# Third attention of a graph network: edge logits from a node table by one-hot products, value rows gathered over three stages

## What is computed

```python
h = (x @ W).reshape(N, HEADS, HEAD_DIM)
a_src = jnp.einsum('nhd,hd->nh', h, att_src)
a_dst = jnp.einsum('nhd,hd->nh', h, att_dst)
e = a_src[src] + a_dst[dst]
e = jax.nn.leaky_relu(e, NEG_SLOPE)
m = jax.ops.segment_max(e, dst, num_segments=N)
e = jnp.exp(e - m[dst])
denom = jax.ops.segment_sum(e, dst, num_segments=N)
alpha = e / denom[dst]
msg = alpha[:, :, None] * h[src]
out = jax.ops.segment_sum(msg, dst, num_segments=N)
return out.reshape(N, HEADS * HEAD_DIM) + bias
```

## Time and profile before

| what | us |
|---|---|
| median of 3 runs | 6803.33 (6801.85 to 6805.95) |
| the profiled execution | 6809.68 |
| its span in the trace | 6807.9 |
| logits of the third attention (`edge_logits`) | 4129 to 4657 |
| its `segment_max` and `bulk` | 4657 to 4712 |
| its `edge_sum` | 4712 to 4962 |

### The profile page before, as it was taken

The page is one execution under the profiler, slowest core; times in us unless marked ns, Lnnn a source line. Parts: engine busy times, 40 slices in busy tenths (PEclk is TensorE's granted clock), DMA queues, the critical chain, the costliest instruction groups (busy, mean ns, idle before and its releaser), DMA issues. The chain is left out here.

```text
span 6807.9 us, 82209 instructions
## 1 busy us (share of the span) xinstructions
PE 4906.5 (72%) x21980; PEld 3937.2 (58%) x21981; DVE 2933.0 (43%) x7123; ACT 1436.9 (21%) x3790; POOL 3441.3 (51%) x3131
## 2 busy tenths in 40 slices
PE   3877486998656486999996754333926588688858
PEld 2777365776444264888886654333626466566645
DVE  5655674323444474101102022114752477567754
ACT  1000482332000192000000221002913122122221
POOL 1777685777577481000000235774833377667710
PEclk8555697999877698999997875556958799789978
DMA  3999461001699673444453546884716388678810
GB/s 116 355 345 323 134 222 46 1 1 18 231 336 339 205 244 100 125 126 125 128 147 102 185 144 193 236 236 152 241 64 201 106 267 260 197 229 261 265 48 24
DMA packets 802690, 1204.72 MB, mean 177 GB/s; under 512 B 102860, under 2 KB 589677, under 8 KB 802313
## 3 DMA queue, kind: packets, MB, share of 16 engines
q1 hardware_dynamic: 365913, 512.77, 25.5%
q0 software_dynamic: 141376, 372.59, 18.8%
q10 hardware_dynamic: 295152, 316.45, 13.2%
HBM read 832.49 MB, written 368.52 MB: 176 GB/s over the span
## 5 line engine op out<-in xcount | busy, mean ns | idle before, releaser
L630 POOL DMA_INDIRECT logit_rows<-tab,src_a x832 | 825.9, 993 | 308.9 <-issue 230.5
L1900 POOL DMA_INDIRECT max_rows<-tab,src_r x784 | 741.1, 945 | 366.6 <-issue 220.3
L749 PE MATMUL ps_a<-msg,sel 128*128 128x264 f32 (+2 forms) x2496 | 621.9, 400 | 132.3 <-DVEq L681 72.2
L1571 POOL DMA_INDIRECT moe_x<-xn,slot x100 | 97.2, 972 | 1219.2 <-POOLq L96 1189.3
L379 POOL DMA_INDIRECT counts<-put_n,put_at x400 | 560.8, 1402 | 215.7 <-issue 135.0
L749 PEld LDWEIGHTS ps_a<-msg,sel 128*128 128x128 f32 x2496 | 454.2, 192 | 299.7 <-DVE acc L695 85.6
L1121 PE MATMUL ps_a<-hl,blocks 128*128 128x256 f32 x2600 | 578.1, 380 | 0.5 <-PE ps_a L1121 0.3
L1121 PEld LDWEIGHTS ps_a<-hl,blocks 128*128 128x128 f32 x2600 | 493.1, 190 | 76.9 <-issue 13.6
L660 POOL TENSOR_TENSOR msg<-edge_rows,extra 128x1024 f32<-128x1024 f32 x208 | 394.0, 1904 | 198.5 <-DMA edge_rows<-slot_rows 124.0
L630 POOL DMA_INDIRECT logit_rows<-tab_kv,src_a x416 | 395.8, 952 | 177.5 <-issue 117.0
L2006 DVE TENSOR_TENSOR_SCAN run<-same,run,ps_t 128x512 f32<-128x512 bf16 x392 | 479.1, 1265 | 0.8 <-PE ps_t L1941 0.8
(11 more groups left out here) (434 smaller groups left out, 9115.0 us busy)
## 6 DMA issues: line engine op xcount, KB each, us to landing
slot_rows<-logit_rows ACTq DMA_DIRECT2D x312, 512.0 KB
edge_rows<-slot_rows SPq DMA_DIRECT2D x312, 512.0 KB
blocks<-counts SPq DMA_DIRECT2D x390, 320.0 KB
seg_rows<-back ACTq DMA_DIRECT2D x196, 512.0 KB
counts<-zeros ACTq DMA_DIRECT2D x130, 320.0 KB
locs<-loc_slots SPq DMA_DIRECT2D x312, 128.0 KB
wf<-in_L_ffn_W SPq DMA_DIRECT2D x57, 512.0 KB
att<-in_attr_t SPq DMA_DIRECT2D x196, 128.0 KB
```

The costliest lines, as they stand in the source:

```text
L630: self.nc.gpsimd.indirect_dma_start(out=self.rows[:, (n % Q) * Q + j, :], out_offset=None, in_=table, in_offset=bass.IndirectOffsetOnAxis( ...
L749: nc.tensor.matmul(ps_a[:, n % 8, 0:C], sel[:, b % 2, j, :], rhs, start=True, stop=True).then_inc(summed, 1)
L1900: nc.gpsimd.indirect_dma_start(out=rows[:, b * Q + j, :], out_offset=None, in_=table, in_offset=bass.IndirectOffsetOnAxis(ap=g.src_r[:, n ...
```

## The change

`edge_logits` is no longer used by `gnn2`. In its place `table_logits` gets a_src of an edge without gathering a row. For a step it makes a one-hot `from_t` of the source's low 7 bits (from a new slot table `slo_slots`), and PE multiplies it with the whole node table `a_s`, 25 tiles by 4 heads: 100 columns. DVE then picks the tile that the source's high bits name (`choose`, against `lane`) and sums over the tiles (`gather_up`). ACT makes `from_t` in two instructions (|s - p|, then ReLU(1 - that)), DVE makes `sel_t` as before.

The rows h are still gathered, by the same 416 indirect DMAs, now of 256 numbers from `tab`, with SP storing each group to `slot_rows`. They are spread over three stages by `LATE = (66, 75)`: groups 0 to 65 in the logits stage, 66 to 74 in `segment_max`, 75 to 103 in the new `late_sum`, which takes the place of `edge_sum`. There POOL gathers 12 groups while DVE does all products of the first 24 groups; from group 24 on POOL does the product of each third group, and gathers one group ahead of it while any is left.

```diff
+LATE = (66, 75)
...
+                o.then(v.tensor_scalar(slo_i[:], ids_i[:, :, 0, :], P - 1, None, ALU.bitwise_and))
                 o.link(v.tensor_copy(ids_f[:], ids_i[:]))
+                o.link(v.tensor_copy(slo_h[:], slo_i[:]))
...
+class Late:
+    def gather(self, pool, n):
+        b = n % Q
+        if n >= Q:
+            pool.wait_ge(self.kept[b], 16 * (n // Q))
+        for j in range(Q):
+            self.nc.gpsimd.indirect_dma_start(
...
+            ).then_inc(self.got[b], 16)
+    def store(self, sp, n):
+        b = n % Q
+        sp.wait_ge(self.got[b], 64 * (n // Q) + 64)
+        sp.dma_start(self.g.slot_rows[n], self.rows[:, b * Q:(b + 1) * Q, :].rearrange("p j d -> p (j d)")).then_inc(self.kept[b], 16)
...
+def table_logits(nc, g, late, gathers, a_s, node_cols, logits, second):
...
+                for n in range(gathers):
+                    late.gather(pool, n)
...
+                for n in range(SG):
+                    b = n % Q
+                    if n >= Q:
+                        sp.wait_ge(sel_set, n - Q + 1)
+                    sp.dma_start(locs[:, b, :], ...
+                    if n >= Q:
+                        sp.wait_ge(far_set, n - Q + 1)
+                    sp.dma_start(slos[:, b, :], ...
+                    while kept < min(gathers - 1, (n - 6) * gathers // SG):
+                        late.store(sp, kept)
+                        kept += 1
...
+                    pe.wait_ge(sel_set, n + 1)
+                    pe.wait_ge(from_set, n + 1)
+                    if n >= 2:
+                        pe.wait_ge(chosen, n - 1)
+                        pe.wait_ge(summed, n - 1)
+                    for j in range(Q):
+                        nc.tensor.matmul(ps_a[:, n % 2, j * NT * H:(j + 1) * NT * H], from_t[:, n % 2, j, :], table, start=True, stop=True)
+                        ins = nc.tensor.matmul(ps_b[:, n % 2, j * P:j * P + 2 * H], sel_t[:, n % 2, j, :],
...
+                select(0)
+                for n in range(SG):
+                    if n + 1 < SG:
+                        select(n + 1)
+                    choose(n)
+                    if n:
+                        leak(n - 1)
+                    gather_up(n)
+                    add(n)
+                leak(SG - 1)
...
+def late_sum(nc, g, late, have, acc, extra, heads):
+    FIRST, AHEAD = 24, 12
+    by_pool = [n >= FIRST and n % 3 == 2 for n in range(SG)]
...
+                for n in range(SG):
+                    if n == FIRST - 1:
+                        for done in range(have, min(have + AHEAD, SG)):
+                            late.gather(pool, done)
+                        done = min(have + AHEAD, SG)
+                    if by_pool[n]:
+                        if done < SG:
+                            late.gather(pool, done)
+                            done += 1
+                        pool.wait_ge(rows_in[n % Q], 16 * (n // Q) + 16)
+                        if n >= 2:
+                            pool.wait_ge(summed, 4 * (n - 2) + 4)
+                        product(nc.gpsimd, n).then_inc(msg_p, 1)
...
+                multiply(0)
+                v.memset(acc[:, :, 0:C], 0.0).then_inc(zeroed, 1)
+                v.memset(odd[:], 0.0).then_inc(zeroed, 1)
+                dve.wait_ge(zeroed, 2)
+                for n in range(SG):
+                    if n + 1 < SG:
+                        multiply(n + 1)
+                    add(n)
...
-def segment_max(nc, g, logits, maxima, H, puts=(0, 0)):
+def segment_max(nc, g, logits, maxima, H, puts=(0, 0), late=None, gathers=(0, 0)):
...
+                    for n in range(*gathers):
+                        late.gather(pool, n)
...
-        node_rows(nc, g, [g.x], [(g.ins["L2_gnn_W"], 0, 0)], D + 8, None, [(0, D + 4, hw, g.tab4), (D + 4, D + 8, adst, None)], ln=True,
+        node_rows(nc, g, [g.x], [(g.ins["L2_gnn_W"], 0, 0)], D + 8, None,
+                  [(0, D, hw, g.tab), (D, D + 4, a_s, None), (D + 4, D + 8, adst, None)], ln=True,
...
-            edge_logits(nc, g, g.tab4, D + 4, cols, logits, 0, D, second=loop_e)
-            segment_max(nc, g, logits, shift, 4)
+            table_logits(nc, g, late, LATE[0], a_s[:], cols, logits, loop_e)
+            segment_max(nc, g, logits, shift, 4, late=late, gathers=LATE)
...
-        edge_sum(nc, g, None, acc, extra, heads=4)
+        late_sum(nc, g, late, LATE[1], acc, extra, heads=4)
```

More of the change, by code:

```diff
@@ L225, in slot_tables @@
         row_i = sb("row_i", [P, STEPS], I32)
+        slo_i, slo_h = sb("slo_i", [SPG, GROUPS, P], I32), sb("slo_h", [SPG, GROUPS, P], BF16)
         turned = ps("turned", [P, 2, 512])
@@ L243, in _ @@
                 sp.dma_start(g.loc_slots.rearrange("(g p l) -> p g l", g=GROUPS, l=P), loc_h[:]).then_inc(loc_out, 16)
+                sp.dma_start(g.slo_slots.rearrange("(g p l) -> p g l", g=GROUPS, l=P), slo_h[:]).then_inc(loc_out, 16)
                 sp.dma_start(g.dst_slots[1:SLOTS + 1].rearrange("(g p l) -> p g l", g=GROUPS, l=P),
@@ L255, in _ @@
                 sp.wait_ge(sent, 96)
-                sp.wait_ge(loc_out, 16)
+                sp.wait_ge(loc_out, 32)
             @block.vector
@@ L916, in _, with __init__ @@
                         ins.then_inc(made, 1)
-def segment_max(nc, g, logits, maxima, H, puts=(0, 0)):
+class Late:
+    def __init__(self, nc, ph, g):
+        self.nc, self.g = nc, g
+        self.rows = ph.sb("late_rows", [P, W, D], F32)
+        self.got = [ph.sem(f"late_got{b}") for b in range(Q)]
+        self.kept = [ph.sem(f"late_kept{b}") for b in range(Q)]
+    def gather(self, pool, n):
[4 more added lines that the diff above has]
+            self.nc.gpsimd.indirect_dma_start(
+                out=self.rows[:, b * Q + j, :], out_offset=None, in_=self.g.tab,
+                in_offset=bass.IndirectOffsetOnAxis(ap=self.g.src_a[:, n * Q + j:n * Q + j + 1], axis=0)
+            ).then_inc(self.got[b], 16)
[3 more added lines that the diff above has]
+        sp.dma_start(self.g.slot_rows[n], self.rows[:, b * Q:(b + 1) * Q, :].rearrange("p j d -> p (j d)")).then_inc(self.kept[b], 16)
@@ L947, in _ @@
                     put_counts(nc, g, pool, *puts)
+            if late is not None:
+                @block.gpsimd
+                def _(pool):
+                    for n in range(*gathers):
+                        late.gather(pool, n)
             @block.sync
@@ L953, in _ @@
                     sp.dma_start(cut[c * H:(c + 1) * H, :], at.partition_broadcast(H)).then_inc(cut_in, 16)
+                if late is not None:
+                    for n in range(gathers[0] - 1, gathers[1] - 1):
+                        late.store(sp, n)
                 sp.wait_ge(cut_in, 16 * C)
@@ L1808, in gnn2 @@
         sb = ph.sb
-        hw = sb("hw", [P, NT, D + 4], F32)
+        hw = sb("hw", [P, NT, D], F32)
         cols = sb("cols", [P, NT, 8], F32)
+        a_s = sb("a_s", [P, NT, 4], F32)
         extra = sb("extra", [P, STEPS, 9], F32)
-        adst, loop, a_s, rows = cols[:, :, 0:4], cols[:, :, 4:8], hw[:, :, D:D + 4], hw[:, :, 0:D]
-        node_rows(nc, g, [g.x], [(g.ins["L2_gnn_W"], 0, 0)], D + 8, None, [(0, D + 4, hw, g.tab4), (D + 4, D + 8, adst, None)], ln=True,
+        late = Late(nc, ph, g)
+        adst, loop, rows = cols[:, :, 0:4], cols[:, :, 4:8], hw[:]
+        node_rows(nc, g, [g.x], [(g.ins["L2_gnn_W"], 0, 0)], D + 8, None,
+                  [(0, D, hw, g.tab), (D, D + 4, a_s, None), (D + 4, D + 8, adst, None)], ln=True,
                   heads=(4, [g.ins["L2_gnn_att_src"], g.ins["L2_gnn_att_dst"]]))
-        bulk(nc, [("v", lambda v: v.tensor_add(loop, a_s, adst)),
+        bulk(nc, [("v", lambda v: v.tensor_add(loop, a_s[:], adst)),
                   ("v", lambda v: v.scalar_tensor_tensor(loop, loop, 0.2, loop, ALU.mult, ALU.max))])
@@ L1840, in gnn2 @@
                   ("v", lambda v: v.tensor_copy(g.seg_end[:], end[:].rearrange("p t a -> p (t a)"))),
-                  ("v", lambda v: v.tensor_tensor(a_s, loop, none[:].broadcast_to([P, NT, 4]), ALU.mult)),
-                  ("v", lambda v: v.tensor_add(shf, shf, a_s)),
+                  ("v", lambda v: v.tensor_tensor(a_s[:], loop, none[:].broadcast_to([P, NT, 4]), ALU.mult)),
+                  ("v", lambda v: v.tensor_add(shf, shf, a_s[:])),
                   ("v", lambda v: v.tensor_sub(loop, loop, shf)),
@@ L2437, in build @@
         g.loc_slots = dram("loc_slots", [SLOTS], BF16)
+        g.slo_slots = dram("slo_slots", [SLOTS], BF16)
         g.same_slots = dram("same_slots", [SLOTS], BF16)
@@ L2444, in build @@
         g.tab8 = dram("tab8", [NP_, D + 8])
-        g.tab4 = dram("tab4", [NP_, D + 4])
         g.slot_rows = dram("slot_rows", [STEPS // Q, P, Q * D])
```

188 lines of the change are left out of this document (added).

## The result

| | us |
|---|---|
| before, median of 4 runs | 6804.64 (6801.85 to 6808.52) |
| after, median of 4 runs | 6700.47 (6693.92 to 6706.78) |
| after / before | 0.9842, 95% interval 0.983 to 0.9854 |
| the profiled execution of after, and its span | 6706.78, 6705.0 |

A forecast was written before the change was run, and what follows sets the result against it. POOL's 416 gathers were taken to limit the logits stage, 520 of 528 us. Terms -162 + 20 + 43 + 3 = -96 took the profiled 6809.7 to 6714, or 6708 since that execution lay 6.35 above the median; range 6660 to 6778.

The forecast's parts named there:

- Step of PE, 3.45 us a group: Logits stage: weight loads set PE's step, 16 records at 0.215 us, so PE sets the pace at 3.45 us a group.
- Rival 3: Logits stage: PE steps as in the first attention's alternating 128- and 64-row weights, 4.19 us a group; total 6785; 8%.
- Rival 4: Logits stage: each wide record adds its stream to its weight load, 4.96 us a group; total 6864, slower; 3%.
- Clock 0.50: Logits stage: PE, though busy all the time, stays at clock 0.50, the 1.2 GHz level.
- rival 1: Logits stage: PE's clock goes up, POOL's 330 us become the bound, stage 338 us, total 6680; 25%.
- DVE beside PE, 2.4 to 2.9 us: Logits stage: DVE's one-hot, choosing, sum and hand-overs take 2.4 us a group, at most 2.9, beside PE's 3.45.
- The order: Logits stage: next group's one-hot made ahead of choosing lets PE start at once; without it DVE's 2.4 us would be added.
- Logits stage, 366 and -162: Logits stage: 104 groups at PE's 3.45 us give 366 us against 528, minus 162 us.
- SP's queue, nothing: Logits stage: SP's broadcasts queue behind stores that wait for gathers; costed at nothing, with 0.4 us cover a store.
- Maximum, +20: Maximum: 36 gathers, some standing still during scans, make the part end at 59 us instead of 38.5, plus 20 us.
- Sum, +43: Sum: DVE's added products and POOL's gathers make it 293 us against 250, plus 43, 22 to 67 by the bounds.
- Small parts, +3: `node_rows` and slot tables: one more ACT instruction a tile, 2.5 us, and two DVE instructions, 1 us; summed as 3.

The follow-up runs named there:

- the wide experiments: Changed kernel with both products of a step zero-padded to 128 columns: 6675.98 us on chip A, 7321.05 on B; also with LATE = (62, 67): 6651.71 on A.
- Variants with 20 gathers: Changed kernel with LATE = (70, 75): 7363.18 us on chip B, 7360.48 on C; with LATE = (62, 67) and both products 128 columns wide: 6651.71 on A.
- quarter stores: Changed kernel storing only a quarter of the gathered rows from group 75 on, output not the reference's: 7336.92 us on chip C, 0.9954 of before.

## Why the prediction was right

The sum was -96, the result -104, and the forecast case is the one that came. The four terms miss by 4.2, 0.4, 3.3 and 0.1 us and all but the second to the same side, so none of them hides another. The mechanism of the logits stage, PE's step at the low clock with everything else beside it, is shown by the experiments on chip A; the division of the sum's term is not. By its steps:

- **Step of PE, 3.45 us a group.** Measured 3.41. The choice of the burst over the alternating pair was right, and the wide experiments show that columns up to 128 cost nothing in it. Rival 3 (4.19) falls. Rival 4, a stream that adds to its load, falls with it. Why the alternating pair of the earlier trace rows steps by 0.26 a record stays open: the prediction put it down to the weights of 64 rows, and no run tried that.
- **Clock 0.50.** Right, in 355 us of unbroken work. That was the best-founded doubt, with 25% on the other side, and the experiments show how near it was: with both products wide the stage of rival 1 came, 344 us against the 338 it gave. The Trainium skill (TensorE: Matmul & The Clock Gate, Part 1) has the clock set by how busy PE has been, with sustained matmuls raising it. Here busy 354.84 of 355 us stayed low and 220.74 of 315 ran at 0.92, so "busy" as a profile counts it does not tell which.
- **DVE beside PE, 2.4 to 2.9 us.** 2.5: it idles 0.91 of 3.42. The total was right from errors that cancel, which is luck. A choosing instruction takes 0.23 (0.313 long, four of them 1.00), not 0.175. `gather_up` takes 0.87: the bound for the strided read, 1.0, was nearer than the 0.5 taken. The four hand-overs of 0.1 each do not show: DVE stands only once a group, for PE. All this is still under PE's time. In the wide versions DVE is at 0.80 to 0.84, so there they begin to count.
- **The order.** The prediction said that without it DVE's 2.4 us would be added. Measured (541.0 - 368.5)/104 = 1.66 a group: of DVE's work only choosing, the one-hot and the hand-overs stand on the path, the sum over tiles does not.
- **Logits stage, 366 and -162.** 369.5 and -166.2. Both of its numbers are short by some us: the part lasts 535.7 before the change, not the 528 of the window in the earlier trace rows, which leaves out 7.7 at its ends, and 3.5 more than forecast after it.
- **SP's queue, nothing.** Right on chip A: POOL waits 35 us for stores and nobody waits for POOL. On chips B and C it waits 161 us and more, and the stage is slower for a reason that stays open.
- **Maximum, +20.** +20.4. Four gathers were held at four scans, as taken from the earlier trace rows. Variants with 20 gathers give 40.4 to 40.8, so 16 gathers cost 19 us and 20 cost about 1. The Trainium skill (GPSIMD Engine Reference, Key points) names DVE instructions with two SBUF inputs as those that contend; the rows agree for the scans, by 2.3 to 2.7 us a gather, and that section gives no size. The aside "5 if scans held nothing" does not come out of its own numbers: 45 us of gathers against a chain of 38.5 are at least 6.5, and with the measured 10 us of the four held gathers taken off the 20.4, some 10 would be left.
- **Sum, +43.** +39.7. First addition 20.1 after the start (19 taken), groups 0 to 23 at 2.6 (2.65), triples with gathers 8.1 to 8.2 (8.1), those without 6.6 (6.8). The 8.1 was put together otherwise than it is: a gather takes 1.109 + 0.30 = 1.41 in the mean, as taken, and the product 1.98, but POOL's products also wait 18.6 us over the 17 triples for PE to free a buffer. "POOL the one waited for" came only in part, as PE waits more for DVE's products (11.4) than for POOL's (8.5). The prediction did not split its 43 us: 26 triples at its own 6.8 would be 271 us, so 21 were DVE's new products and 22 the gathers. The runs point to less of the first and more of the second: without gathers the stage took 250.2 on chip B against 241.7 in the kernel before by the same marks (4713.37 to 4955.05, on a chip like A), and the gathers cost 42 on chip B. Since the chips differ, the split on chip A stays open, and that the term came out near is in part luck.
- **Small parts, +3.** +2.9 up to the logits stage, but not where it was put: `node_rows` with its 25 extra ACT instructions did not grow, and the slot tables take 1.5 (1 taken). The rest came mostly in the stages between these two, in code that the change does not touch. It is in the size of run to run, and the agreement is chance.

## What to carry to other kernels

Where PE does many small products, count the steps of records, not columns: at the low clock 8, 100 and 128 columns cost the same step here, and the choice of width decided the clock. Before a gain is credited to what was removed, look at the order in which the other engines issue their work on the next group: here the order alone was worth 172 us of the logits stage, in a change that brings 104. And what is taken off one engine as a whole should be placed by asking, stage by stage, who has time: the maximum could take 20 gathers for 1 us, the next 16 cost 19, and in the sum 116 and the shift of products to DVE cost 40. Last, repeat a comparison only against a run on the same chip: the order was worth 172 us of this stage on one chip and 56 on another.

## What the runs showed of the hardware that was not expected

- Padding the products with zeros, by 28 and by 120 columns, made the stage 24 us shorter (368.5 to 344.4), with the granted clock at 0.92 instead of 0.50.
- Between chips the same kernel (that before) took 6802 and 7376 us, 8.4% apart. Of the variants, the same stretch had 345 and 285 GB/s, at DMA shares of 1.03 and 0.89, and only the slower chips have waits for a sender that the profile does not name. The changed kernel's margin is smaller on those chips: its neighbour with quarter stores has a ratio of 0.9954 there, against 0.9837. A schedule in which one engine paces a stage on one chip can be paced by other waits on another.
- A reduction that reads 400 numbers with a stride of four took 0.87 us, 2.2 ns a number, where the reduction of 1664 adjacent bf16 numbers in the maximum (`cut`, L1320) took 1.89, 1.1 ns a number. Type and stride differ at once, so which of them does it is open.
